# Attention and expert layer on one core: a batch's context loaded one batch sooner, and its picks placed ahead of two heads' scaling

## The reference

```
x = x + attention(layernorm(x), ctx)        # q = x wq, k = ctx wk, v = ctx wv, softmax, wo, b_o
g = softmax(layernorm(x) @ router_w + router_b);  two best experts of each token
pos = cumsum(chosen) - 1;  a token is kept where pos < capacity (640)
x = x + sum over its experts of g * (gelu(xn @ w1 + b1) @ w2 + b2)
```

## Time and profile before

| what | value |
|---|---|
| median of 3 runs | 1069.85 us (1066.33 to 1071.13) |
| profiled execution, its own time | 1072.4 us |
| span of that execution, first to last instruction | 1070.2 us |
| mean granted TensorE clock | 0.971 |
| PE busy | 974.9 us (91%) |
| DVE busy | 775.1 us (72%) |
| ACT busy | 627.5 us (59%) |
| POOL busy | 258.9 us (24%) |

### The profile page before, as it was taken

The page is one execution under the profiler, slowest core; times in us unless marked ns, Lnnn a source line. Parts: engine busy times, 40 slices in busy tenths (PEclk is TensorE's granted clock), DMA queues, the critical chain, the costliest instruction groups (busy, mean ns, idle before and its releaser), DMA issues. The chain is left out here.

```text
span 1070.2 us, 22859 instructions
## 1 busy us (share of the span) xinstructions
PE 974.9 (91%) x8224; PEld 875.9 (82%) x8224; DVE 775.1 (72%) x2096; ACT 627.5 (59%) x1738; POOL 258.9 (24%) x428
## 2 busy tenths in 40 slices
PE   4789999999999998999999999999753999999996
PEld 3678888888888887888888788888543999999996
DVE  4777778788777877878787878878543777766662
ACT  3777767667767766677676667767412344443330
POOL 2320211222231222223132222311232222223332
PEclk9899999999999999999999999999965999999998
DMA  8530100011010101101010100000024144455522
GB/s 222 152 88 2 31 1 31 22 31 51 2 50 13 32 13 31 32 11 41 7 35 6 31 16 23 26 4 12 11 95 169 20 124 125 123 128 130 129 26 25
DMA packets 47822, 56.73 MB, mean 53 GB/s; under 512 B 5228, under 2 KB 43098, under 8 KB 47584
## 3 DMA queue, kind: packets, MB, share of 16 engines
q1 hardware_dynamic: 38880, 46.30, 13.9%
q0 software_dynamic: 8832, 8.98, 5.3%
HBM read 36.01 MB, written 24.20 MB: 56 GB/s over the span
## 5 line engine op out<-in xcount | busy, mean ns | idle before, releaser
L732 ACT ACTIVATE prob<-psum,negmax 128x256 f32<-128x256 f32 x512 | 241.6, 489 | 116.9 <-DVE negmax L889 116.9
L686 ACT ACTIVATE probt<-psum 128x512 f32<-128x512 f32 x256 | 160.3, 630 | 45.6 <-PE psum L566 44.6
L889 DVE TENSOR_REDUCE negmax<-psum 128x2 f32<-128x512 f32 x256 | 158.7, 683 | 21.3 <-PE psum L550 21.2
L900 DVE TENSOR_SCALAR prob<-prob,invtot 128x256 f32<-128x256 f32 x512 | 164.3, 384 | 4.5
L566 PE MATMUL psum<-ident,prob 128*128 128x128 f32 x1024 | 153.2, 273 | 1.2 <-DVE prob L900 1.1
L813 ACT ACTIVATE hid<-psum,b1t 128x640 f32<-128x640 f32 x64 | 50.9, 796 | 136.6 <-PE psum L487 136.6
L566 PEld LDWEIGHTS psum<-ident,prob 128*128 128x128 f32 x1024 | 120.3, 142 | 11.4 <-issue 1.8
L580 PE MATMUL psum<-probt,v 128*64 128x256 f32 x1024 | 128.3, 394 | 0.8 <-ACT probt L686 0.8
L439 POOL DMA_INDIRECT slot_table<-row,picki x64 | 65.5, 1023 | 200.9 <-DVE picki L1002 174.9
L732 ACT ACTIVATION_READ_ACCUMULATOR prob<-psum,negmax 128x1 f32 x512 | 113.1, 221 | 0.0
L467 POOL DMA_INDIRECT out_rows<-y,rowi x40 | 65.5, 1638 | 185.9 <-DVE y L1051 163.7
(11 more groups left out here) (155 smaller groups left out, 2670.7 us busy)
## 6 DMA issues: line engine op xcount, KB each, us to landing
w1r<-in_w SPq DMA_DIRECT2D x8, 1024.0 KB, 8.1
w2r<-in_w SPq DMA_DIRECT2D x8, 1024.0 KB
slot_table<-blank SPq DMA_DIRECT2D x8, 662.5 KB, 9.5
rows<-slot_table SPq DMA_DIRECT2D x8, 662.5 KB, 5.3
xin<-in_x SPq DMA_DIRECT2D x16, 256.0 KB, 2.9
out_rows<-x SPq DMA_DIRECT2D x16, 256.0 KB, 3.2
c<-in_ctxt SPq DMA_DIRECT2D x16, 128.0 KB, 3.0
c<-in_ctxt SPq DMA_DIRECT2D x32, 64.0 KB, 2.9
```

What stands on the lines that cost most here:

```text
L686: copy = lambda dst, src, **kw: act.activation(dst, src, ACT.Copy, **kw)
L732: last = act.activation(prob[:, m % 2, u, qb, :], psum[:, u, qb * S:(qb + 1) * S], ACT.Exp, bias=negmax[:, m % 2, u, qb:qb + 1], accum_out ...
L889: dve.tensor_reduce(negmax[:, m % 2, u, :], psum[:, u, :].rearrange("p (q s) -> p q s", q=ST), AX.X, ALU.max, negate=True).then_inc(sem("m ...
L900: last = dve.tensor_scalar(prob[:, m % 2, u, qb, :], prob[:, m % 2, u, qb, :], invtot[:, m % 2, u, qb:qb + 1], None, ALU.mult)
```

## The change

The split and use of the context stay where they are. `load_ctx(2)` is issued ahead of SP's loop, and in the loop `load_ctx(b + 3)` takes the place of `load_ctx(b + 2)`. The step `pick` of batch b - 3 moves in the list from behind `v` to ahead of `inv0`, `norm0` and `norm1`, in the period r = 3 of a batch. The number of instructions and transfers is the same.

```diff
@@ timeline(), inside the loop over periods
         out += [("k", m + 1)] if more else []
+        out += [("pick", b - 3)] if r == 3 and 3 <= b < B else []
         out += [("inv0", m), ("norm0", m), ("norm1", m)] if live else []
@@
         if 3 <= b < B:
-            out += {0: [("gate", b - 3), ("rank", b - 3)], 3: [("pick", b - 3)]}.get(r, [])
+            out += [("gate", b - 3), ("rank", b - 3)] if r == 0 else []
@@ SP
+            load_ctx(2)
             for b in range(B):
-                if b + 2 < B:
-                    load_ctx(b + 2)
+                if b + 3 < B:
+                    load_ctx(b + 3)
                 sp.wait_ge(sem("x2"), ST * (b + 1))
```

## The result

The changed kernel takes 1074.47 us (median of 5 runs, 1072.42 to 1075.88), and the kernel before 1069.58 us (5 runs, 1066.33 to 1071.13). The ratio is 1.0056, with an interval of 1.0038 to 1.0074. So in this pair of measurements the change made the kernel slower by half a per cent, where 1.4% faster was forecast. Later measurements of the same two kernels, further down, came out the other way.

A forecast was written before the change was run, and what follows sets the result against it. PE, busy 91%, was taken as the bound, losing time through the late context. From the median 1069.85 us, -16.0 + 1.6 = -14.4 us gave 1055.5 us, with an 8 in 10 range of 1051 to 1062.

The forecast's parts named there:

- The context: Period r = 2, batches 4 to 14: earlier context ends DVE's wait for the inverse root; gain 16.0 us, bounds 14.2 and 16.
- ACT's stand: ACT idle before `qh` in eleven places, each in an r = 0, reason given only as remote; 16.8 us in all.
- I put it at zero, with 2 us to either side: r = 0: effect of POOL's scatter moving by 1.26 us on ACT's remote idle time before `qh`, taken as nothing.
- The picks: DVE, r = 3: moved ahead of the scaling, which ends 1.03 us later at no cost; at most 1.03 us a batch.
- The split beside DVE: r = 0: POOL's split slows DVE's scaling; 0.15 us a batch of PE time, 1.6 us in all, at most 12.8.
- the first rival: Split slows DVE in r = 0, reaching the maxima of r = 1; at half the bound 1060.3 us; chance 0.16.
- The Trainium skill's rule on the shared access: POOL shares SBUF access with VectorE; the scaling and `gate` comparisons near the split suffer, speaking against the change; no separate size.
- The slower one: r = 0: DVE stands still through the whole split, 2.9 us a batch, 32 us in all; time 1086 us; chance 0.03.
- That the change should fail to free POOL: POOL: the context wait hides another with the same end, such as k and v; time near 1069.9 us; chance 0.05.

The follow-up runs named there:

- the half scatter: The changed kernel with two of the four indirect transfers of each scatter, second experts' rows left out: 1052.7 us in one run, 1051.42 us in another.
- the second pair: Both kernels once more, unchanged, on another chip: changed kernel 1053.33 us, kernel before 1056.84 us, ratio 0.9966.
- the hold: One ACT copy held until POOL issued the scatter's fourth transfer, batches 5 to 15: changed kernel 1066.74 us, kernel before 1062.52, early context alone 1057.32.

## Why the prediction was wrong

**The context: right where it was worked out.** The chain from SP's issue to PE's two waits was read rightly, and its price in that pair of profiles was right to a tenth: eleven windows of 12.54 us, 137.92 against 137.94. What the text missed is why the context was late. It took x2's time as given, and x2 was late by 1.6 us, together with ACT's stand. Without the stand only 1.4 us were to be won in r = 2 (139.27 less 137.9), and the whole change wins 3.5 us (0.34%). Where the other 2 us come from the profiles don't show: up to batch 4 alone, single executions of these kernels differ by up to 6 us (196.75 to 202.59 us over all profiles).

**The step that failed** is "I put it at zero, with 2 us to either side". The stand of ACT, given as remote, moved from `qh` to `ah`, and that cost 17.6 us. The row was there, the text saw that POOL's scatter was under way then and would move by 1.26 us, and it didn't ask what stands behind the other instruction on which the stand could fall. Behind `qh` stand steps with slack: r = 0 was 12.28 us with the stand there and 12.10 without. Behind `ah` stand `al`, `bias` and the bank of `k`, with 0.3 us of slack: a copy 2.09 us late made r = 0 1.78 us longer in the first profile of the change, and one 1.51 us late by hand made it 1.21 us longer.

Rows of the kernel before would have given this rival a price. There the stand ends at 396.01 in batch 8, and ACT's copy of the attention output starts at 393.01.

```profile
393.01 0.60 ACT L686 ACTIVATE ah<-psum 128x512 fp32r<-128x512 f32 x1 [1.34 <-PE psum L580]
```

Were the end to move by 1.26 us with the scatter, to 394.75, and to bind this copy, it would be 1.74 us late. Eleven times that is 19 us, an estimate with hindsight, and the forecast of 1055.5 would have become some 1075.

**The picks.** On DVE they cost nothing, as forecast: the picks alone measured 0.9996 (0.9978 to 1.0013). They cost through POOL's scatter only if the stand follows it, which isn't shown. For that speak the two first profiles. The stand before `qh` ends at 396.01 (one of the eleven in the earlier trace rows), 0.88 us after the end of the scatter's fourth issue in the kernel before:

```profile
394.15 0.98 POOL L439 DMA_INDIRECT slot_table<-row,picki  x1 [0.30 <-issue]
```

The stand before `ah` ends at 393.04, 0.79 us after the end of that issue in the changed kernel:

```profile
391.27 0.98 POOL L441 DMA_INDIRECT slot_table<-row,picki  x1 [0.30 <-issue]
```

The eleven places are the periods in which a scatter other than the first is issued. This is a coincidence in time, in two profiles. It wasn't shown that the scatter makes the stand, since the half scatter ran only where there was none.

**The split beside DVE: small in the time by two errors that cancel.** The term was 0.15 us a batch, 1.6 us in all: a delay of 0.2 to 0.5 us on DVE, less 0.15 of slack. In the changed kernel without the stand, more than the end of the split met DVE's work. The bias on POOL began only 0.31 us sooner in batch 8 (7.12 us into r = 0 against 7.43), not 1.26, since POOL waited 2.19 us for the scatter to land instead of 1.24. So the whole split lay beside the scaling and the steps of `gate`:

```profile
390.47 1.68 DVE L902 TENSOR_SCALAR prob<-prob,invtot 128x256 f32<-128x256 f32 x4
...
395.17 0.42 DVE L922 TENSOR_TENSOR x<-psum,xin 128x256 f32<-128x256 f32 x1
```

DVE reached x2 1.16 us into r = 1 instead of 0.05, so the delay was 1.1 us. And yet r = 0 kept its 12.10 us and r = 1 its 10.35, so the slack was as large. That the term came out near right is luck. With the old place of the picks and a late q the slack is used up, and it costs 3.7 us in ten periods, the first rival's mechanism. The Trainium skill's rule on the shared access (GPSIMD Engine Reference, section 1, Specifications) agrees with the 2.38 us here. It wasn't the rule that decided the result.

**The rivals.** The slower one had the wrong mechanism: DVE lost 1.1 us beside a split of 3.1 us, not all of it, and that cost PE nothing. That the change should fail to free POOL didn't come about either.

**What stays open.** What ACT waited for in the first two profiles isn't known, nor what differs there. The same program runs 13 to 21 us faster in the later measurements (the changed one 1074.47 against 1053.08 to 1054.79 us, the one before 1069.58 against 1053.81 to 1056.84). It looks more like late signs of PE than like a busy ACT, for two reasons. In the first profile of the kernel before, the copy `ah` too started late, 4.07 us into r = 0 where it starts at 3.62 in the second, in ten of the eleven batches, and the profile puts that wait down to PE, which had gone on to `q` 0.58 us before (0.12 us in the second pair). And in the first profile of the change DVE too waited for PE, for the third maximum, just as POOL issued the third transfer (389.99), and it didn't so in the second profile of the same kernel. But these are more rows of the same kind, not a proof. Which part of the change is to blame where the stand exists was tried with the hold alone: with it, the change takes 1066.74 us and the early context without the moved picks 1057.32 us, on the same chip, with the hold before `ah` in the one and before `qh` in the other, as the two first profiles have it. So the early context alone is the better version of the two if the real stand would stay before `qh` with it, which no run shows. Without the stand it measured 0.9973 and the change 0.9966, intervals that overlap.

## What to carry to other kernels

A wait whose releaser the profile doesn't name isn't a wait without a price: ask on which instruction it would fall if the work beside it moves, and count what stands behind that instruction, above all a bank in turn that PE needs next. Before a late transfer is loaded sooner, follow its lateness back to the first cause, since it may go away, or stay, with that cause. And where a profile has an unexplained stall, work out the gain of a change with and without it, and measure both kernels on more than one chip.

## What the runs showed that was not expected

One program, without a change, takes 1069.58 us in the first measurement and 1053.81 to 1056.84 us on four chips later, and what differs in the profiles is ACT's stand in eleven periods and what follows from it. Of the 16.5 us between the two profiles of the kernel before (spans of 1070.2 and 1053.7), 14.7 lie in r = 2 and 1.9 in r = 0, less 0.1 us elsewhere. Of the 21.2 us between those of the changed kernel (1072.7 and 1051.5), 19.5 lie in r = 0. The granted clock was 0.971 before and 0.968 after in the first pair, and 0.969 and 0.971 in the second, and it was 1.00 in the periods compared, so it isn't the clock.
